# One PSUM bank per kind of product, one small product per tick, and state sums in four parts

## The chip, the cores and the metric

One core of one Trainium2 chip. The metric is the device time of the whole program in microseconds. Of the kernel before, three runs are shown: median 8285.81 us, 8284.54 to 8287.15. The chip's engines are called PE (TensorE, matmuls), DVE (VectorE), ACT (ScalarE), POOL (GpSimd) and SP (SyncE, which issues nearly all DMAs here). PSUM has eight banks of 128 partitions by 512 fp32.

## The reference, cut to what matters

Sixteen images of 64 channels by 64x64 pixels go through two layers.

```python
# layer 0
y = leaky_relu(conv3x3(x)); y = leaky_relu(conv3x3(y))
seq = y as 4096 tokens of 64 channels
x, z = split(seq @ in_proj_w)                 # 128 channels each
x = silu(conv1d(x))                           # 4 taps along the tokens
dt, B, C = split(x @ x_proj_w)                # 4, 16, 16
delta = softplus(dt @ dt_proj_w + dt_proj_b)
h = exp(delta * A) * h + (delta * x) * B      # a scan over 4096 tokens, 128 channels x 16 states
y = sum over states of h * C, + x * D
seq = (y * silu(z)) @ out_proj_w              # back to 64 channels
# layer 1
out_c = softmax(xc @ xc.T) @ x                # attention over channels
out_s = v @ softmax(q.T @ k).T                # attention over 4096 x 4096 positions
out   = x + w_bn @ concat(out_c, out_s)
```

## The kernel before, in words

The convolutions run first, by themselves, up to about 590 us. The rest is one software pipeline written out by hand, in **ticks**. An image is 8 chunks of 512 tokens. A chunk has 16 ticks, one for each group of 8 channels x 16 states, and so an image has 128 ticks. `T` counts ticks, and `r = T % 16` is the place in the chunk. In this text "r8" means the tick with r = 8 in each chunk. The 16 images are run as two spans of eight (`SPANS`), with a barrier between them. Each engine has its own loop over T, and takes its work in the order of that loop; semaphores tie the loops together.

In a tick T these things are done:

- SP fetches `lanes` for tick T+3 (`AHEAD`): 512 KB of `delta` and `delta*x`, spread over partitions (line 755). It waits for the slot of tick T-1 to be free.
- ACT takes `exp` of the lanes into `dA` for tick T+1 (line 1042). DVE multiplies lanes by B into the bank `DBU` (line 1159, "dbu" below), and scans (line 1170) into a ring `hst` of 24 slots. POOL multiplies the state of the tick before by C (line 1264, `hc_in`).
- The **search** for the largest score runs one image behind the scan: PE makes two products from keys and queries, `dif` and `max` (line 868). ACT takes a Relu of `dif` into `gains` (line 988), and DVE folds `max` and `gains` into a running maximum (line 1113), one tick after the Relu. Four key blocks of an image are loaded into `kx` (`SEARCH_LOAD`, line 709). The last of them needs the last chunk's keys, which `st_split` stores (lines 769 and 771).
- The **attention** runs `MAIN` ticks behind: PE makes two score products `S` (line 936), ACT takes their `exp` into `pr` (line 1036), PE multiplies the `pr` of the tick before by the values ("PV", line 947, eight instructions) and in every even tick sums two ticks' `pr` ("SUM", line 962, eight instructions).

Besides, each chunk needs **small products** of PE, each read by ACT or DVE: `xin` and `z` (lines 888, 890, 886), `dt` (894), `BC` (898), `y` (the sum of the states over 16 slots, 32 instructions, line 909), `out` (904), `xv` (917) and `en` (922). Every 32 ticks there are `turn` (874) and `res` (882), and once an image `mix` (878). `small_uses(T)` says which fall in a tick; before, `y` is in r2 as one block, and r0 holds both `xin` and `z`.

Five banks (`RING`) are handed out in turn to all of these, in the order in which PE writes them: `bank_of` is `number[e] % RING`. PE waits for the reader of the product five places before. Within a tick, `plan(T)` gives PE the order `dif`, S, S, `max`, PV, SUM, small products. ACT begins a tick with the Relu of `dif`, then the two `exp` of S, then `dA`, then waits for that tick's small products. DVE's further work of a chunk stands after `max` in its ticks: the gates (lines 1181 and 1186), the softplus (1192, 1194 in r7; 1200, 1203 in r9), the key difference (1209 in r8), the low part of the keys and queries (1215 in r10), and every 32 ticks `accs` (1221), the multiplication by the reciprocal (1231) and `res` (1135). ACT's `Ln` in r8 is between two loads of its function table.

The softplus result goes through `spread_d` in DRAM (`st_sp`, lines 729 and 732), and B and C through `bc_d` (`st_bc`, `ld_b`, `ld_c`, lines 738 to 746).

Of the kernel before, what the change touches and what calls it, by code (L numbers as in the profile page):

```python
# [19 lines left out]
ALU = mybir.AluOpType  # L20
# [3 lines left out]
P = 128  # L24
# [17 lines left out]
BLOCK = 32  # L42
# [68 lines left out]
class Span:  # L111
# [7 lines left out]
    def __init__(self, j, images, tail):  # L119
# [4 lines left out]
        self.uses, self.number, self.freed = [], {}, {}  # L124
        self.counts = {}
        for T in range(self.first, self.last):
# [70 lines left out]
    def small_uses(self, T):  # L197

        ev = []
        found, last = self.searches(T), self.searches(T - 1)  # L200
        if found:
            ev.append(("dif", found, (T - SEARCH) % KT))
        if last:
            ev.append(("max", last, (T - 1 - SEARCH) % KT))
# [3 lines left out]
        a = self.channel(T, MAIN + 14)  # L208
        if a is not None:
            ev.append(("mix", a))  # L210
        done = self.ended(T - 13)
# [3 lines left out]
        for name in {0: ("xin", "z"), 6: ("dt",), 10: ("BC",)}.get(r, ()):  # L215
            if self.chunk(sl + 1):
                ev.append((name, sl + 1))
        name = {2: "y", 7: "out", 12: "xv", 14: "en"}.get(r)
        if name and self.chunk(sl - 1):
            ev.append((name, sl - 1))  # L220
        return ev

    def plan(self, T):

        uses = self.small_uses(T)
        plan = [e for e in uses if e[0] == "dif"]
# [7 lines left out]
        return plan + [e for e in uses if e[0] not in ("dif", "max")]  # L234
# [203 lines left out]
def pipeline(nc, banks, seq_d, scratch, w_z, w_x_t, cw, cb, w_dt_t, w_dt, dt_b, w_bc, a_log, skip,  # L438
# [4 lines left out]
    with ExitStack() as ctx:  # L443
# [143 lines left out]
        def span(j, images, tail, i):  # L587
# [33 lines left out]
            def bank_of(e):  # L621
                return RB[number[e] % RING]
# [12 lines left out]
            for T in range(sched.first, sched.last):  # L635
# [13 lines left out]
                if sched.chunk(c):  # L649
                    for at, n in ((4, "tanh"), (5, "z_tanh"), (5, "gated"),  # L650
                                  (6, "z_gated"), (6, "abs_in"), (6, "em_in"), (7, "em1_in"),
                                  (8, "ln_in"), (9, "delta_in"), (9, "du_in"), (10, "st_sp"),
                                  (11, "st_bc"), (12, "ld_b"), (12, "ld_c")):
                        if r == at:
                            sched.note(n, c)
                if r == 6 and sched.chunk(c + 2):
# [5 lines left out]
                if sched.chunk(c):  # L662
                    for at, n in ((4, "y2_in"), (8, "st_x1"), (8, "kd_in"), (9, "head_in"),
                                  (10, "low_in"), (14, "st_split"), (13, "st_vt")):
                        if r == at:
                            sched.note(n, c)
                for n, offset in (("max_in", TURN - 1), ("nm_in", TURN), ("nm_row", TURN + 1), ("acc_in", MAIN + KT),
# [20 lines left out]
            with nc.Block() as block:  # L688
                @block.sync
                def _(sp):  # L690
# [29 lines left out]
                    for T in range(first, last):  # L720
                        sl, r = T // GROUPS, T % GROUPS
                        c = sl + 1
                        if r == 6 and sched.chunk(c + 2):
                            full_wait(sp, ("z", c))
                            load_seq(c + 2)
                        if sched.chunk(c) and r == 10:
                            if due("delta_in", c):
                                sp.wait_ge(S["delta_in"], due("delta_in", c))
                            issued(sp.dma_start(spread_d[c % 2, :, 0, :], dsp[:]), "st_sp")
                            if due("du_in", c):  # L730
                                sp.wait_ge(S["du_in"], due("du_in", c))
                            issued(sp.dma_start(spread_d[c % 2, :, 1, :], usp[:]), "st_sp")
                        if sched.chunk(c) and r == 11:
                            taken(sp, ("BC", c))
                            wait(sp, "ld_b", c - 2, 16)
                            wait(sp, "ld_c", c - 2, 16)
                            for j in range(BLOCKS):
                                issued(sp.dma_start(bc_d[c % 2][:, P * j:P * (j + 1)],
                                                    bcs[BLOCK * j:BLOCK * (j + 1), :]), "st_bc")
                        if sched.chunk(c) and r == 12:  # L740
                            wait(sp, "st_bc", c, 16 * BLOCKS)
                            wait(sp, "dbu_in", GROUPS * (c - 1) - 1)
                            issued(sp.dma_start(bbc[:, c % 2, :], bc_d[c % 2, 0:D_STATE].unsqueeze(1).broadcast_to(
                                [D_STATE, DL, CHUNK])), "ld_b")
                            wait(sp, "hc_in", GROUPS * (c - 1) - 1)
                            issued(sp.dma_start(cbc[:, c % 2, :], bc_d[c % 2, D_STATE:].unsqueeze(1).broadcast_to(
# [575 lines left out]
```

## Time and profile before

| | us |
|---|---|
| median of three runs | 8285.81 |
| the profiled execution: its own time | 8273.81 |
| the profiled execution: span of its instructions | 8272.0 |
| convolutions and loading, up to the first scan | 591 |
| scans alone (first image) | 591 to 1079 |
| scans, search and attention together | 1079 to 7843 |
| attention of the last image, and the end | 7843 to 8272 |

The page gives busy shares of the whole span: PE 91%, DVE 77%, ACT 70%, POOL 41%. Its line of the granted TensorE clock, in 40 slices of 207 us and in tenths of full speed, shows 8, 6, 6, 8 in the third to the sixth slice and 9 in all others. A matmul's end is modelled, so the starts of matmuls are what to read, not their busy time. In a row of the timeline the numbers are the start in us, how long the group took, and in brackets how long the engine had stood idle, and what ended that.

### The profile page before, as it was taken

How to read it: one execution, taken by the hardware profiler on the slowest of the kernel's cores; microseconds unless marked ns; L12 is line 12 of the kernel's file. 1: busy time of each engine (PE TensorE's matmuls, PEld its weight loads, DVE VectorE, ACT ScalarE, POOL GpSimd, SP SyncE). 2: the span in 40 equal slices, each digit the busy share in tenths (PEclk: the TensorE clock that was granted, in tenths of full speed). 3: DMA queues.
4: the chain of work that ended last, by engine and by line, in shares of the span. 5: the costliest groups of instructions: out<-in, count | busy, mean ns of one | idle time of the engine just before them, and what ended most of it. 6: DMA issues, size and time to landing. Idle time of an engine off the chain costs nothing. (4 is left out here: it accounts for less than half of the span.)

```text
span 8272.0 us, 143757 instructions
## 1 busy us (share of the span) xinstructions
PE 7526.8 (91%) x44622; PEld 2839.9 (34%) x44622; DVE 6384.9 (77%) x10331; ACT 5779.3 (70%) x10216; POOL 3397.1 (41%) x4134
## 2 busy tenths in 40 slices
PE   9963489999999999999989999999999999999999
PEld 2321133333333333333333333333333333333333
DVE  2228888888888888888878888888888888888831
ACT  1124477777877778777777777777778777787765
POOL 0015544444444444444444444444444444444400
PEclk9986689999999999999999999999999999999999
DMA  9838878888787878787877888788787878888710
GB/s 152 134 91 218 222 198 203 208 201 207 196 209 202 200 201 205 203 207 200 204 187 201 206 204 208 195 205 207 200 206 195 209 200 202 204 201 203 184 36 12
DMA packets 856720, 1555.81 MB, mean 188 GB/s; under 512 B 401288, under 2 KB 419472, under 8 KB 855952
## 3 DMA queue, kind: packets, MB, share of 16 engines
q1 hardware_dynamic: 853904, 1546.08, 76.2%
q8 instruction: 355, 5.82, 0.3%
q14 instruction: 413, 3.38, 0.2%
q10 hardware_dynamic: 2048, 0.53, 0.0%
HBM read 1335.21 MB, written 193.74 MB: 185 GB/s over the span
## 5 line engine op out<-in xcount | busy, mean ns | idle before, releaser
L1264 POOL TENSOR_TENSOR hst<-hst,cbc 128x512 f32<-128x512 f32 x2048 | 2618.2, 1278 | 3575.8 <-DVE bank L1159 3553.5
L1170 DVE TENSOR_TENSOR_SCAN hst<-dA,carry,bank 128x512 f32<-128x512 f32 x1792 | 2294.2, 1280 | 142.6 <-issue 36.6
L1036 ACT ACTIVATE pr<-bank 128x512 f32<-128x512 f32 x4096 | 2224.3, 603 | 40.2 <-PE bank L936 38.8
L947 PE MATMUL bank<-pr,vt 128*32 128x512 f32 x16384 | 2244.9, 621 | 0.0
L868 PE MATMUL bank<-kx,qr 96*128 96x512 f32 x4096 | 2046.6, 501 | 201.3 <-DMA kx<-kx_d 90.8
L988 ACT ACTIVATE gains<-bank 128x512 f32<-128x512 f32 x2048 | 1222.3, 597 | 994.3 <-PE bank L868 702.3
L1042 ACT ACTIVATE dA<-lanes,small 128x512 f32<-128x512 f32 x2048 | 1502.5, 734 | 524.5 <-DMA lanes<-spread_d 492.6
L1159 DVE TENSOR_TENSOR bank<-lanes,bbc 128x512 f32<-128x512 f32 x2048 | 1517.7, 741 | 264.3 <-DMA lanes<-spread_d 237.9
L1113 DVE CUSTOM_DVE_ANT_0 gains<-bank,gains 128x512 f32<-128x512 f32 x2048 | 1371.0, 669 | 388.5 <-PE bank L868 382.2
L936 PE MATMUL bank<-qr,kr 98*128 98x512 f32 x4096 | 1392.4, 413 | 184.3 <-ACT pr L1036 164.2
L868 PEld LDWEIGHTS bank<-kx,qr 96*128 96x128 f32 x4096 | 782.0, 191 | 1597.4 <-issue 1003.9
L962 PE MATMUL bank<-pr,ones 128*32 128x512 f32 x8192 | 1130.8, 625 | 16.6 <-ACT dens L1051 15.9
L936 PEld LDWEIGHTS bank<-qr,kr 98*128 98x128 f32 x4096 | 784.4, 192 | 529.2 <-ACT pr L1036 287.1
L947 PEld LDWEIGHTS bank<-pr,vt 128*32 128x32 f32 x16384 | 324.9, 108 | 702.4 <-issue 692.4
L909 PE MATMUL bank<-hst,cst 128*32 128x512 f32 x4096 | 481.9, 612 | 64.6 <-POOL hst L1264 64.6
L962 PEld LDWEIGHTS bank<-pr,ones 128*32 128x32 f32 x8192 | 274.3, 115 | 690.2 <-issue 624.4
L1257 POOL COPY carry<-hst 128x1 f32<-128x1 f32 x1792 | 473.4, 264 | 66.6 <-DVE hst L1170 60.5
L407 ACT ACTIVATE biased<-bank,bias 128x512 f32<-128x512 f32 x128 | 81.0, 684 | 452.9 <-PE bank L395 442.5
L1151 DVE SCALAR_TENSOR_TENSOR ysb<-u,small,bank 128x512 f32<-128x512 f32 x128 | 95.5, 746 | 390.6 <-PE bank L909 390.6
L1170 DVE TENSOR_TENSOR_SCAN hst<-dA,bank 128x512 f32<-128x512 f32 x256 | 312.5, 1221 | 11.7 <-ACT dA L1042 0.5
L1277 POOL TENSOR_TENSOR usp<-dsp,u 128x512 f32<-128x512 f32 x128 | 211.8, 1655 | 266.2 <-DVE dsp L1203 266.2
L909 PEld LDWEIGHTS bank<-hst,cst 128*32 128x32 f32 x4096 | 136.1, 114 | 395.1 <-issue 394.4
(114 smaller groups left out, 5118.9 us busy)
## 6 DMA issues: line engine op xcount, KB each, us to landing
lanes<-spread_d SPq DMA_DIRECT2D x2048, 512.0 KB, 6.4
seqt<-seq_d SPq DMA_DIRECT2D x256, 128.5 KB, 4.9
spread_d<-dsp SPq DMA_DIRECT2D x128, 256.0 KB, 2.0
spread_d<-usp SPq DMA_DIRECT2D x128, 256.0 KB, 2.0
bbc<-bc_d SPq DMA_DIRECT2D x128, 256.0 KB, 3.9
cbc<-bc_d SPq DMA_DIRECT2D x128, 256.0 KB, 4.5
kx<-kx_d SPq DMA_DIRECT2D x192, 128.0 KB, 4.8
qr<-parts_d SPq DMA_DIRECT2D x192, 128.0 KB, 4.8
```

The source lines that it names most:

```text
L868: mm = nc.tensor.matmul(bank[:].rearrange("p (c n) -> p c n", n=HALF), qr[0:SPLIT, ring_slot((a, q)), nt * P:(nt + 1) * P].bitcast(F32R), ...
L909: mm = nc.tensor.matmul(bank[BLOCK * j:BLOCK * (j + 1), :], cst[:, C_SUM + BLOCK * gl:C_SUM + BLOCK * (gl + 1)], hst[:, slot_of(GROUPS * c ...
L936: nc.tensor.matmul(bank[:], kr[0:rows, t * P:(t + 1) * P].bitcast(F32R), qr[0:rows, ring_slot((a, q)), cols].bitcast(F32R), start=True, st ...
L947: mm = nc.tensor.matmul(ACC[CH * h + o:CH * h + o + BLOCK, :], vt[:, t, o:o + BLOCK], pr[:, T % PRING, h, :], start=t == 0, stop=t == KT - ...
L962: mm = nc.tensor.matmul(DEN[o:o + 32, :], ones[:], pr[:, (2 * p + par) % PRING, h, :], start=t == 1, stop=t == KT - 1, tile_position=(0, o))
L988: nc.scalar.activation(gains[:, k % 2, :], bank_of(e)[:], ACT.Relu).then_inc(S["act_took"], 1)
L1036: nc.scalar.activation(pr[:, T % PRING, h, :], bank_of(("S", T, h))[:], ACT.Exp).then_inc(S["p_full"], 1)
L1042: nc.scalar.activation(dA[:, (T + 1) % 2, :], lanes[:, (T + 1) % SLOTS, 0, :], ACT.Exp, scale=amat[:, g:g + 1]).then_inc(S["da_in"], 1)
L1113: nc.vector.tensor_tensor_reduce(out=gains[:, k % 2, :], in0=bank[:], in1=gains[:, k % 2, :], scale=1.0, scalar=LOWEST, op0=ALU.add, op1=A ...
L1159: nc.vector.tensor_tensor(DBU[:], lanes[:, T % SLOTS, 1, :], bbc[:, sl % 2, :], ALU.mult).then_inc(S["dbu_in"], 1)
L1170: nc.vector.tensor_tensor_scan(hst[:, slot_of(T), :], dA[:, T % 2, :], DBU[:], carry[:, g:g + 1] if sl % CHUNKS else 0.0, ALU.mult, ALU.ad ...
L1264: nc.gpsimd.tensor_tensor(h, h, cbc[:, (T - 1) // GROUPS % 2, :], ALU.mult).then_inc(S["hc_in"], 1)
```

## The change

It does four things.

1. `bank_index` gives each kind of product a bank of its own: `dif` 0, `max` 1, the two S 2 and 3, all small products 4. PE waits for the reader of the product that was in the bank before (`prior`).
2. At most one small product stands in a tick, and its reader (ACT or DVE) takes it in the next tick. The new places: `xin` r1, `z` r2, `out` r3, `dt` r4, `xv` r5, `BC` r6, `en` r7, `res` or `turn` r8, `mix` r9. ACT begins a tick with the small product of the tick before, then the two `exp`, then the Relu. PE begins a tick with S.
3. `y` is written in four parts, eight instructions each, in r13, r14, r15 and r0, into one bank; DVE reads the sum in r1.
4. What follows moves along: gates r3 and r4, softplus r6 and r8, key difference r5, `head` r6, low part r7, `Ln` r7, the stores `st_bc` r8, `st_sp` and `st_split` r9, loads of B and C r10. SP fetches `lanes` before anything else of a tick. `MAIN` goes from 32 to 30, the search from -6 to -9, and the last `kx` load from tick 16 to tick 9 of the next image, where it stands behind the `st_split` of the same tick.

```diff
-MAIN = 32
-SEARCH = -6
+MAIN = 30
+SEARCH = -9
-END = 14
+RES = 10
+MIX = 57
+END = RES + 2
+SPLIT_AT = 9
-SEARCH_LOAD = [SEARCH - KT + 8 * (p + 1) + 1 for p in range(QUARTERS - 1)] + [GROUPS]
+SEARCH_LOAD = [SEARCH - KT + 8 * (p + 1) + 1 for p in range(QUARTERS - 1)] + [SPLIT_AT]
...
-                self.number[e] = len(self.uses)
-                self.uses.append(e)
+                self.number[e] = len(self.number)
+                self.prior[e] = held.get(bank_index(e))
+                held[bank_index(e)] = e
+                if e[0] == "y" and e[2] < GPB - 1:
+                    continue
...
-        for name in {0: ("xin", "z"), 6: ("dt",), 10: ("BC",)}.get(r, ()):
-            if self.chunk(sl + 1):
-                ev.append((name, sl + 1))
-        name = {2: "y", 7: "out", 12: "xv", 14: "en"}.get(r)
+        name = {1: "xin", 2: "z", 4: "dt", 6: "BC"}.get(r)
+        if name and self.chunk(sl + 1):
+            ev.append((name, sl + 1))
+        name = {3: "out", 5: "xv", 7: "en"}.get(r)
         if name and self.chunk(sl - 1):
             ev.append((name, sl - 1))
+        c, part = (sl - 1, GPB - 1) if r == 0 else (sl, r - GROUPS + GPB - 1)
+        if 0 <= part and self.chunk(c):
+            ev.append(("y", c, part))
+        assert len(ev) <= 1
         return ev
...
-        uses = self.small_uses(T)
-        plan = [e for e in uses if e[0] == "dif"]
-        if self.attends(T):
-            plan += [("S", T, 0), ("S", T, 1)]
-        plan += [e for e in uses if e[0] == "max"]
+        plan = [("S", T, 0), ("S", T, 1)] if self.attends(T) else []
+        plan += self.search_uses(T)
         if self.attends(T - 1):
             plan.append(("PV", T - 1))
         if T % 2 == 0 and self.attends(T - 1):
             plan.append(("SUM", T // 2 - 1))
-        return plan + [e for e in uses if e[0] not in ("dif", "max")]
+        return plan + self.small_uses(T)
+
+def bank_index(e):
+    return {"dif": 0, "max": 1, "S": 2 + e[-1] if e[0] == "S" else 0}.get(e[0], 4)
...
             def bank_of(e):
-                return RB[number[e] % RING]
+                return RB[bank_index(e)]
...
-                        if number[e] >= RING:
-                            taken(pe, sched.uses[number[e] - RING])
+                        if sched.prior[e]:
+                            taken(pe, sched.prior[e])
...
-                            wait(pe, "hc_in", GROUPS * (c + 1) - 1)
-                            for gl in range(GPB):
-                                for j in range(BLOCKS):
...
+                            gl = e[2]
+                            wait(pe, "hc_in", GROUPS * c + BLOCKS * (gl + 1) - 1)
+                            for j in range(BLOCKS):
...
@@ ACT, one tick
-                        near = [e for e in sched.small_uses(T) if e[0] == "dif"]
-                        for e in near:
-                            small_use(e)
+                        for e in sched.small_uses(T - 1):
+                            if e in number:
+                                small_use(e)
                         if sched.attends(T):
...
+                        for e in sched.search_uses(T):
+                            small_use(e)
                         if sched.spreads(T + 1):
...
-                        for e in sched.small_uses(T)[len(near):]:
-                            small_use(e)
```

## Rows read from the trace of the kernel before

**Rows 1.** Busy time by stage: us, then each engine, granted clock, DMA share, GB/s.
```profile
591.00:1079.00 488.00, 195.40 (x682) 81.22 (x682) 403.83 (x493) 221.55 (x335) 270.09 (x320) 0.62 0.87 219
1079.00:7843.00 6764.00, 6393.21 (x38247) 2449.67 (x38248) 5736.16 (x9328) 5225.91 (x9278) 3114.59 (x3772) 0.97 0.81 202
7843.00:8272.00 429.00, 408.09 (x2586) 146.69 (x2585) 109.45 (x305) 240.30 (x456) 3.82 (x3) 0.98 0.09 23
```

**Rows 2.** Timeline of DVE over one chunk: the scans of r4, r7 to r13.
```profile
4017.96 1.28 DVE L1170 TENSOR_TENSOR_SCAN hst<-dA,carry,bank 128x512 f32<-128x512 f32 x1
...
4027.42 1.28 DVE L1170 TENSOR_TENSOR_SCAN hst<-dA,carry,bank 128x512 f32<-128x512 f32 x1
...
4031.01 1.28 DVE L1170 TENSOR_TENSOR_SCAN hst<-dA,carry,bank 128x512 f32<-128x512 f32 x1
...
4034.10 1.28 DVE L1170 TENSOR_TENSOR_SCAN hst<-dA,carry,bank 128x512 f32<-128x512 f32 x1
...
4037.95 1.28 DVE L1170 TENSOR_TENSOR_SCAN hst<-dA,carry,bank 128x512 f32<-128x512 f32 x1
...
4042.10 1.28 DVE L1170 TENSOR_TENSOR_SCAN hst<-dA,carry,bank 128x512 f32<-128x512 f32 x1
...
4045.38 1.28 DVE L1170 TENSOR_TENSOR_SCAN hst<-dA,carry,bank 128x512 f32<-128x512 f32 x1
...
4047.89 1.28 DVE L1170 TENSOR_TENSOR_SCAN hst<-dA,carry,bank 128x512 f32<-128x512 f32 x1
```

**Rows 3.** Timeline of PE over the same chunk, from `y` in r2 to r12.
```profile
4010.36 3.62 PE L909 MATMUL bank<-hst,cst 128*32 128x512 f32 x32
...
4016.38 0.64 PE L936 MATMUL bank<-qr,kr 98*128 98x512 f32 x2
...
4019.38 0.63 PE L936 MATMUL bank<-qr,kr 98*128 98x512 f32 x2
...
4021.51 0.64 PE L936 MATMUL bank<-qr,kr 98*128 98x512 f32 x2
...
4025.37 0.63 PE L936 MATMUL bank<-qr,kr 98*128 98x512 f32 x2
...
4034.51 0.51 PE L936 MATMUL bank<-qr,kr 98*128 98x512 f32 x1 [0.24 <-ACT gains L988]
4036.42 0.79 PE L936 MATMUL bank<-qr,kr 98*128 98x512 f32 x1 [1.40 <-ACT pr L1036]
...
4037.63 1.94 PE L947 MATMUL bank<-pr,vt 128*32 128x512 f32 x8
...
4040.36 0.39 PE L898 MATMUL bank<-u,wbc 128*32 128x128 f32 x8
...
4042.71 0.38 PE L874 MATMUL bank<-cst,mx 128*8 128x128 f32 x2
...
4043.36 0.63 PE L936 MATMUL bank<-qr,kr 98*128 98x512 f32 x2
```

**Rows 4.** Waits from 1079 to 7843 us: total us, times, longest.
```profile
DVE ysb L1151 <- PE bank L909: 379.5, 117, 7.0
...
ACT xv L1024 <- PE bank L917: 94.1, 86, 1.5
...
PE bank L868 <- DMA kx<-kx_d: 80.6, 14, 7.7
```

**Rows 5.** PE's timeline after one of those waits for `kx`.
```profile
4253.51 0.77 PE L868 MATMUL bank<-kx,qr 96*128 96x512 f32 x1 [6.12 <-DMA kx<-kx_d]
```

**Rows 6.** Waits of SP's queue, 1079 to 7843 us: total, times, longest.
```profile
SPq L729 <- DVE dsp L1203: 605.6, 117, 5.7
...
SPq L604 <- DMA kx_d<-low: 72.1, 13, 6.2
```

**Rows 7.** The page's list of DMA issues: KB each, median us to landing.
```profile
lanes<-spread_d SPq DMA_DIRECT2D x2048, 512.0 KB, 6.4
```

**Rows 8.** Waits from 591 to 1079 us, scans alone.
```profile
DVE bank L1159 <- DMA lanes<-spread_d: 70.0, 25, 12.1
```

More of the change, by code:

```diff
@@ L199, in small_uses @@
         ev = []
[L200 to L204, printed above, removed]
         turned = self.quarter_at(T, TURN)
@@ L649, in span @@
                 if sched.chunk(c):
[L650 to L653, printed above, removed]
+                    for at, n in ((2, "tanh"), (3, "z_tanh"), (3, "gated"),
+                                  (4, "z_gated"), (5, "abs_in"), (5, "em_in"), (6, "em1_in"),
+                                  (7, "ln_in"), (8, "delta_in"), (8, "du_in"), (9, "st_sp"),
+                                  (8, "st_bc"), (10, "ld_b"), (10, "ld_c")):
                         if r == at:
                             sched.note(n, c)
-                if r == 6 and sched.chunk(c + 2):
+                if r == 4 and sched.chunk(c + 2):
                     sched.note(f"seq{c % 2}", c + 2)
@@ L721, in _ @@
                         sl, r = T // GROUPS, T % GROUPS
[L722 to L736, printed above, removed]
-                            for j in range(BLOCKS):
[L738 to L746, printed above, removed]
-                                [D_STATE, DL, CHUNK])), "ld_c")
                         X = sched.fetches(T)
@@ L756, in _ @@
                                                 near.partition_broadcast(D_STATE)), f"lanes{X % SLOTS}")
+                        c = sl + 1
+                        if r == 4 and sched.chunk(c + 2):
+                            full_wait(sp, ("z", c))
+                            load_seq(c + 2)
+                        if sched.chunk(c) and r == 9:
+                            if due("delta_in", c):
+                                sp.wait_ge(S["delta_in"], due("delta_in", c))
+                            issued(sp.dma_start(spread_d[c % 2, :, 0, :], dsp[:]), "st_sp")
+                            if due("du_in", c):
+                                sp.wait_ge(S["du_in"], due("du_in", c))
+                            issued(sp.dma_start(spread_d[c % 2, :, 1, :], usp[:]), "st_sp")
+                        if sched.chunk(c) and r == 8:
+                            taken(sp, ("BC", c))
+                            wait(sp, "ld_b", c - 2, 16)
+                            wait(sp, "ld_c", c - 2, 16)
+                            for j in range(BLOCKS):
+                                issued(sp.dma_start(bc_d[c % 2][:, P * j:P * (j + 1)],
+                                                    bcs[BLOCK * j:BLOCK * (j + 1), :]), "st_bc")
+                        if sched.chunk(c) and r == 10:
+                            wait(sp, "st_bc", c, 16 * BLOCKS)
+                            wait(sp, "dbu_in", GROUPS * (c - 1) - 1)
+                            issued(sp.dma_start(bbc[:, c % 2, :], bc_d[c % 2, 0:D_STATE].unsqueeze(1).broadcast_to(
+                                [D_STATE, DL, CHUNK])), "ld_b")
+                            wait(sp, "hc_in", GROUPS * (c - 1) - 1)
+                            issued(sp.dma_start(cbc[:, c % 2, :], bc_d[c % 2, D_STATE:].unsqueeze(1).broadcast_to(
+                                [D_STATE, DL, CHUNK])), "ld_c")
                         c = sl - 1
@@ L1060, in _ @@
                         c = sl + 1
-                        if sched.chunk(c) and r == 4:
+                        if sched.chunk(c) and r == 2:
                             taken(act, ("xin", c))
@@ L1076, in _ @@
                             nc.scalar.activation(em[:], em[:], ACT.Exp, scale=-1.0).then_inc(S["em_in"], 1)
-                        if sched.chunk(c) and r == 8:
+                        if sched.chunk(c) and r == 7:
                             if due("em1_in", c):
@@ L1081, in _ @@
                         c = sl - 1
-                        if sched.chunk(c) and r == 9:
+                        if sched.chunk(c) and r == 6:
                             wait(act, "kd_in", c)
@@ L1103, in small_use @@
                         kind, c = e[0], e[1]
-                        if kind not in DVE_USES or kind == "y":
+                        if kind not in DVE_USES or e not in sched.freed:
                             return
@@ L1128, in small_use @@
                                                     ALU.subtract).then_inc(S["nm_in"], 1)
+                        elif kind == "y":
+                            full_wait(dve, ("out", c - 1))
+                            nc.vector.scalar_tensor_tensor(out=ysb[:], in0=u[:, c % 2, :], scalar=dskip, in1=bank[:],
+                                                           op0=ALU.mult, op1=ALU.add).then_inc(S["dve_took"], 1)
                         elif kind == "mix":
@@ L1205, in _ @@
                         c = sl - 1
-                        if sched.chunk(c) and r == 8:
+                        if sched.chunk(c) and r == 5:
                             qk = x1c[CH:P, c % 2, :]
@@ L1210, in _ @@
                                                     ALU.subtract).then_inc(S["kd_in"], 1)
-                        if sched.chunk(c) and r == 10:
+                        if sched.chunk(c) and r == 7:
                             if due("head_in", c):
@@ L1266, in _ @@
                         c = sl - 1
-                        if sched.chunk(c) and r == 4:
-                            taken(pool, ("y", c))
+                        if sched.chunk(c) and r == 2:
+                            taken(pool, ("y", c, GPB - 1))
                             wait(pool, "z_gated", c)
@@ L1272, in _ @@
                         c = sl + 1
-                        if sched.chunk(c) and r == 9:
+                        if sched.chunk(c) and r == 8:
                             if due("delta_in", c):
```

69 lines of the change are left out of this document (33 added, 36 removed).

## The prediction

> **What bounds the kernel now.** I read the busy time by stage first, then the rhythm of the scans on DVE, then the starts of PE's matmuls over the same chunk, and last the waits.
>
> By stage, 6764 of the 8272 us belong to the stretch where scan, search and attention run together [rows 1]. It holds 118 chunks of 16 ticks, so only what happens once a chunk, or once an image there (14 images), can move the time much. PE is busy for 95% of it, DVE for 85%, ACT for 77%; DMA stands at 81%. Three things are near their limit together.
>
> The timelines say how they share it. PE's plain ticks repeat exactly: 2.13 us without SUM, 3.00 with it, and 3.86 where `dt` comes on top, so `dt` is 0.87 [rows 3]. DVE's plain tick is 2.51 us (r12, the last two scans) [rows 2]. So PE is the slower one only where a tick has SUM or a large small product, and DVE where a tick has gates, softplus or key work. Before the change the two kinds of load lie in different places. `y` stands in r2 as one block of 3.62 us [rows 3], `xin` and `z` in r0: there DVE waits (379.5 us for `y` alone [rows 4]) while PE runs without a gap. From r4 to r11 it is the other way round. From the scan of r4 to that of r12 DVE takes 27.43 us [rows 2]; PE's S of the same ticks are 26.98 us apart. PE's own work in these eight ticks is 4 x 3.00 + 4 x 2.13, `dt` and `out` at 0.87 each, `BC` and `turn` at no more than 0.39 and 0.38: 23.0 us [rows 3]. So DVE asks for 4.4 us more than PE, and PE loses 4.0 of them. The slack of about one tick between the engines takes up only 0.4. The loss shows in r10: S stands 0.24 and 1.40 us behind ACT's reads, and then the PV takes 1.94 us [rows 3].
>
> Once an image PE waits 5.8 us for the last `kx` (80.6 us in 14 waits [rows 4]), and the products after it run slow (0.77 us for one search product [rows 5], where two of S, as wide, take 0.63 [rows 3]); with that I call it 7.5 us an image.
>
> **The change part by part.** All sums go against the profiled execution, 8273.81 us.
>
> *Small products of a chunk.* PE issues the same instructions, DVE too, so 51 us of PE work in a chunk stay. What changes is where they meet. `y` costs 3.62 / 4, about 0.9 us, in each of r13, r14, r15 and r0; these ticks and r1 to r4 are now PE's. The ticks in which DVE has more to do are r5 to r9. From the spacing of the scans before [rows 2]: the key difference makes a tick 3.09 us, the first half of softplus 3.59, the second half 3.85, the low part 4.15 (with the reduction of the maximum, which comes in every other chunk; 4.0 without half of it). In r8 `en` is read too, and in every other chunk the reciprocal is multiplied in: I add 0.2 and half of 0.67 (half of what the two operations of the second softplus tick cost, 3.85 - 2.51). In r9 `res` or `turn` is read, 0.7 over 2.51. The sum of r5 to r9 is 3.09 + 3.59 + 4.0 + 4.4 + 3.2 = 18.3 us.
> PE in r5 to r9 has 3 x 2.13 + 2 x 3.00, `xv` at about 0.9, `BC` 0.4, `en` 0.6 (both `xv` and `en` are estimates between `BC` and `dt`), and half of 0.87 + 0.38 for `res` or `turn`: 14.9 us. The excess is 3.4 us. If 0.4 is taken up as before, PE loses 3.0 instead of 4.0 in a chunk. The ends: all of a tick's slack (2.1) could be used, which leaves 1.3; or ACT's table load for `Ln`, now in r7 with `head`, the gates and `xv` in the ticks around it, holds S of r9 longer and the loss stays at 4. I take 3.0, the ratio the rows show.
>
> *Readers in the next tick.* ACT stood 94.1 us behind `xv` [rows 4], 0.8 a chunk, with `dA` of the tick after queued behind it, for which DVE's scan waits. This goes: 0.6 a chunk, between 0 and 0.8. What is late next is the `exp`, which stands behind the read of the small product, but that product ended a tick's S earlier.
>
> So a chunk gains 1.0 + 0.6 = 1.6 us, 118 of them 189 us.
>
> *A bank for each kind.* PE may no longer run five products ahead; each kind must be read before its next tick. In plain ticks this costs nothing: ACT has read S some 1.5 us before PE wants the bank again, under PV. Its cover is gone where ACT is late, which is r8 and r9; there S comes first, and `dif` cannot pass in front of it as it did in r10. That is 0 to 0.5 us a chunk, which the ratio above has in it.
> The Trainium skill, "Perfetto Trace Analysis", section "Matmuls", says that independent matmul groups should rotate through different PSUM banks so that the reading of one overlaps the next group's matmuls. The change does the opposite within a kind. By that rule alone the 1.0 us of r5 to r9 would not come; the trace before, though, has its longest gap just where the ring of five rotates [rows 3]. It is the second rival.
>
> *`y` in parts.* Its first three parts need states that are many ticks old. The last needs POOL's product of r15, which runs while DVE does the dbu and scan of r0; PE comes to it at the end of r0, some 2 us later. Nothing is added, and DVE's wait in r3 goes, but under PE's work, so it buys nothing by itself.
>
> *SP's queue and the last `kx`.* SP waits 605.6 us for the softplus (5.2 a chunk) with the fetch of `lanes` for r13 behind it [rows 6]. In the new order that fetch still stands behind `st_sp`, and now behind four stores of `st_split` too, but the softplus is a tick earlier. `lanes` land 6.4 us after issue [rows 7], and three ticks of about 3 us give 9, so 2.6 us are left; I take 0 for an ordinary chunk.
> The `kx` wait of PE goes: the load is issued in tick 9 for a product of tick 15, some 18 us. But SP must stand there for `st_split` before it can issue the load; this wait is 5.5 us each today (72.1 in 13 [rows 6]), and now the fetch for r13 is queued behind it. 5.5 and 1 for the issues, less the 2.6 that are left: 4 us an image, between 0 (the stores land faster where fewer DMAs run) and 7.5. I take 4, so 3.5 an image are gained, 14 x 3.5 = 49 us.
>
> *First image.* DVE waits 70 us for `lanes` there [rows 8], and DMA stands at 0.87 [rows 1]. The new SP order, without the waits for B and C ahead of the fetch, should give a part: 0 to 40 us, I take 18 (a quarter).
>
> *Start and end.* Two ticks fewer of scan alone (488 / 160 = 3.05 us) and of attention alone (429 / 160, about 2.6, as the end's DMA chain is in it), two more of both together (3.5): 4 us.
>
> Sum: 189 + 49 + 18 + 4 = 260, so 8014 us for an execution like the profiled one. The median of the three runs lies 12 us above that one; 8026, and I say **8025**.
>
> **The rivals.**
>
> *PE's losses nearly vanish.* If the separate banks let all of a tick's slack be used, PE loses 1.3 instead of 4.0: 2.7 + 0.6 = 3.3 a chunk, 389 us, with 49 + 22 more: 460, **7825**. For it: PE loses only where a reader is late, and slow PV after the gap adds to it. Against it: 4.0 of 4.4 were lost so far.
> The Trainium skill, "Perfetto Trace Analysis", section "Identifying the Most-Contended Engine", would go further: matmul busy time is a bad measure, weight loads a good one, and these are busy for 36% of the stretch [rows 1]. By it PE would not be a limit. The exact 2.13 and 3.00 us of PE's ticks speak against it.
>
> *The separate banks give nothing.* PE stands before S of r9 as long as before, and only the `kx` wait, the first image and the ends remain: 49 + 22 = 71, **8215**.
>
> *The fetch for r13 comes late in every chunk.* Place: SP's tick 9, where spread stores, split stores and, right behind, the loads of B and C are put in front of `lanes`. Price: from the point where `lanes` take more than 9 us to land, instead of 6.4, DVE and ACT stand, and after 1.4 us of idle PE also runs slow, as in r10 before (the PV of 1.94 [rows 3]). At 2.7 us a chunk net of the 1.6 gained, 1.1 x 118 = 130, and with `kx` and the first image gaining nothing: **8415**. For it: DMA is at 81%, and SP's `kx` wait shows a store that landed slowly [rows 6]. Against it: the scan's tick before r13 leaves 2.6 us, and DMA runs nearly empty while SP waits for the softplus.
>
> *It doesn't do what it says*: the `kx` wait only moves, and the rest cancels: about 8280.
>
> **How the numbers follow.** Forecast (7890 to 8140) 0.50; losses nearly vanish 0.16; nothing from the banks (8140 to 8269) 0.16; no change 0.05; late fetch 0.13. A change of under 0.2% (17 us) can't be told from none here. Faster: 0.50 + 0.16 + 0.16 = 0.82; same 0.05; slower 0.13. The range for 8 in 10 leaves out the late fetch and the far end of the first rival: 7770 to 8250. The forecast's own range is 7890 to 8140.
>
> **What would show it.** DVE's wait for `y` gone, PE's wait for `kx` gone, PE's S in r13 to r4 spaced by its own work (3.86 in r14 and r0, 3.0 in r13 and r15), and one gap left, in r9, of 1 to 2 us before S. SP waits for `kx_d` in tick 9 of an image, and `lanes` for r13 of that chunk late. Wrong, if DVE or ACT wait for `lanes` at r13 in every chunk, if PE waits at `xin` in r1 for DVE's read of `y`, or if the gap at r9 is longer than 3 us.

## The result, and the profile after

The changed kernel takes 8208.24 us (median of four runs, 8202.77 to 8212.31) against 8285.17 for the kernel before beside it: ratio 0.9909, 95% interval 0.9894 to 0.9924. It is faster, by 0.9%, where 3.1% were forecast (8025 us). The forecast's sign was right, but of the 260 us that it gave, 77 came. The profiled execution took 8212.31 us, 61.5 less than that of before.

Busy time by stage after (us, then each engine as busy time and instructions, granted clock, DMA share, GB/s), against [rows 1]:
```profile
588.00:1079.00 491.00, 222.17 (x693) 72.52 (x693) 398.67 (x492) 220.79 (x335) 269.17 (x316) 0.57 0.86 218
1079.00:7791.00 6712.00, 6384.75 (x38292) 2431.72 (x38289) 5681.32 (x9335) 5174.91 (x9286) 3050.69 (x3777) 0.98 0.81 204
7791.00:8210.00 419.00, 399.21 (x2537) 143.92 (x2535) 105.76 (x297) 236.59 (x449) 3.52 (x3) 0.98 0.09 24
```
The borders are the same events as before: the first scan, the first S, the last scan. The common stage is 52 us shorter, with two ticks more in it. The scans alone gain nothing: the first S stands at 1079 us as before, so 158 ticks take 491 us, 3.11 each, where 160 took 488, 3.05 each. The end is some 9 us shorter.

Waits after from 1073 to 7780 us (in us: total, times, longest), against [rows 4]. Before, the same view gave 167.9 us in 128 waits for DVE behind `lanes`, and 295.8 in 266 for ACT.
```profile
ACT dA L1058 <- DMA lanes<-spread_d: 629.9, 267, 8.0
DVE bank L1170 <- DMA lanes<-spread_d: 471.8, 242, 7.2
PE bank L950 <- ACT pr L1050: 231.1, 195, 5.4
PE bank L882 <- DVE mxp L1127: 62.8, 70, 1.1
DVE ysb L1145 <- PE bank L923: 1.5, 1, 1.5
ACT xv L1038 <- PE bank L931: 0.6, 1, 0.6
```
DVE's wait for `y` (379.5 us) and ACT's for `xv` (94.1) are gone, and no wait of PE for `kx` is left. In their place DVE and ACT wait for `lanes`, some 300 us more each. 242 waits in 118 chunks are two a chunk: the timeline has them at the starts of r13 and r14, on average 1.68 and 1.72 us of DVE's idle time in a chunk that does not begin an image. ACT's rows of one chunk (start, duration, what was done, idle time before it and what ended it):
```profile
4015.22 1.28 ACT L1094 ACT_TABLE_LOAD   x1
4016.51 0.63 ACT L1094 ACTIVATE em<-em 128x512 f32<-128x512 f32 x1
4017.16 1.28 ACT L1050 ACT_TABLE_LOAD   x1
...
4033.01 0.72 ACT L1058 ACTIVATE dA<-lanes,small 128x512 f32<-128x512 f32 x1 [2.42 <-DMA lanes<-spread_d]
...
4037.04 0.72 ACT L1058 ACTIVATE dA<-lanes,small 128x512 f32<-128x512 f32 x1 [1.85 <-DMA lanes<-spread_d]
```
SP's queue in tick 9 of the same chunk says why (start, issue time, what is issued):
```profile
4019.11 0.34 SPq L752 DMA_DIRECT2D spread_d<-dsp  x1
...
4020.85 0.34 SPq L755 DMA_DIRECT2D spread_d<-usp  x1
...
4021.29 0.55 SPq L783 DMA_DIRECT2D parts_d<-head  x1
4021.89 0.55 SPq L783 DMA_DIRECT2D parts_d<-low  x1
4022.47 0.58 SPq L785 DMA_DIRECT2D kx_d<-head  x1
4023.10 0.43 SPq L785 DMA_DIRECT2D kx_d<-low  x1
4023.64 0.81 SPq L743 DMA_DIRECT2D lanes<-spread_d  x1
4024.54 1.26 SPq L766 DMA_DIRECT2D bbc<-bc_d  x1
4025.86 0.95 SPq L769 DMA_DIRECT2D cbc<-bc_d  x1
```
The four stores of the split come between `usp` and the fetch for r13 and take 2.35 us of issue; B and C follow at once. The fetch itself goes out 2.8 us after its slot is free (5.46 before), but it lands 9.34 us after its issue (4.75 before), and `dA` reads it as soon as it has landed, 9.35 us after the issue (6.24 before); these are averages over chunks that don't begin an image. The page's medians over all ticks hide this, except for B's load, which took 3.9 us before:
```profile
lanes<-spread_d SPq DMA_DIRECT2D x2048, 512.0 KB, 6.7
bbc<-bc_d SPq DMA_DIRECT2D x128, 256.0 KB, 9.5
```
PE in r8 to r11, the part that the forecast was to improve [rows 3], and the granted clock (the third value from the end) over the gap:
```profile
4013.89 0.73 PE L950 MATMUL bank<-qr,kr 98*128 98x512 f32 x2
...
4019.11 0.99 PE L950 MATMUL bank<-qr,kr 98*128 98x512 f32 x2 [1.52 <-ACT pr L1050]
...
4021.09 1.94 PE L961 MATMUL bank<-pr,vt 128*32 128x512 f32 x8
...
4022.96 1.06 PE L950 MATMUL bank<-qr,kr 98*128 98x512 f32 x2
...
4026.26 0.73 PE L950 MATMUL bank<-qr,kr 98*128 98x512 f32 x2
```
```profile
4013.50:4019.20 5.70, 4.07 (x31) 1.54 (x29) 5.53 (x12) 5.62 (x8) 1.31 (x2) 1.00 0.67 175
4019.20:4021.00 1.80, 1.80 (x4) 0.64 (x4) 0.77 (x2) 1.80 (x5) 1.75 (x2) 0.80 0.48 164
4021.00:4023.00 2.00, 2.00 (x10) 0.24 (x9) 1.93 (x5) 1.71 (x4) 1.44 (x2) 0.50 0.39 138
```
From S of r8 to that of r11 PE takes 12.37 us, for 8.5 us of work: 3.9 are lost, where 4.0 were lost before. Averaged over ordinary chunks (neither the first nor the second of an image) it is 3.6 for 3.85. PE waits at two places there: 1.25 us for ACT before S of r9, in every chunk, and 0.9 us for DVE's maximum in r10, in 56 chunks of 89.

### The profile page after: what moved, and what is told of

Same layout as the page of the kernel before. It is cut to its first block and busy times, and to the rows that moved or that the text cites. A ratio compares the mean times of both kernels' runs of the same rounds, so it can differ in the third digit from the quotient of the medians.

```text
span 8210.5 us, 143761 instructions
## 1 busy us (share of the span) xinstructions
PE 7535.5 (92%) x44622; PEld 2809.7 (34%) x44622; DVE 6321.3 (77%) x10331; ACT 5724.2 (70%) x10216; POOL 3332.0 (41%) x4134
## 5 line engine op out<-in xcount | busy, mean ns | idle before, releaser
L950 PE MATMUL bank<-qr,kr 98*128 98x512 f32 x4096 | 1724.9, 494 | 240.5 <-ACT pr L1050 231.1
L1170 DVE TENSOR_TENSOR bank<-lanes,bbc 128x512 f32<-128x512 f32 x2048 | 1497.3, 731 | 559.7 <-DMA lanes<-spread_d 536.7
L882 PE MATMUL bank<-kx,qr 96*128 96x512 f32 x4096 | 1444.9, 424 | 105.3 <-DVE mxp L1127 92.8
L1002 ACT ACTIVATE gains<-bank 128x512 f32<-128x512 f32 x2048 | 1249.2, 610 | 29.7 <-DVE mxp L1127 20.1
L950 PEld LDWEIGHTS bank<-qr,kr 98*128 98x128 f32 x4096 | 684.1, 192 | 1591.5 <-issue 865.9
L976 PE MATMUL bank<-pr,ones 128*32 128x512 f32 x8192 | 1087.9, 603 | 0.0
L923 PE MATMUL bank<-hst,cst 128*32 128x512 f32 x4096 | 569.9, 630 | 168.0 <-POOL hst L1274 142.5
L1267 POOL COPY carry<-hst 128x1 f32<-128x1 f32 x1792 | 388.0, 217 | 109.1 <-DVE hst L1181 87.8
L1036 ACT ACTIVATE cacc<-bank,small 128x512 f32<-128x512 f32 x128 | 87.9, 687 | 222.9 <-PE bank L904 221.2
```

What stands on the lines that cost most here:

```text
L882: mm = nc.tensor.matmul(bank[:].rearrange("p (c n) -> p c n", n=HALF), qr[0:SPLIT, ring_slot((a, q)), nt * P:(nt + 1) * P].bitcast(F32R), ...
L923: mm = nc.tensor.matmul(bank[BLOCK * j:BLOCK * (j + 1), :], cst[:, C_SUM + BLOCK * gl:C_SUM + BLOCK * (gl + 1)], hst[:, slot_of(GROUPS * c ...
L950: nc.tensor.matmul(bank[:], kr[0:rows, t * P:(t + 1) * P].bitcast(F32R), qr[0:rows, ring_slot((a, q)), cols].bitcast(F32R), start=True, st ...
L976: mm = nc.tensor.matmul(DEN[o:o + 32, :], ones[:], pr[:, (2 * p + par) % PRING, h, :], start=t == 1, stop=t == KT - 1, tile_position=(0, o))
L1002: nc.scalar.activation(gains[:, k % 2, :], bank_of(e)[:], ACT.Relu).then_inc(S["act_took"], 1)
L1170: nc.vector.tensor_tensor(DBU[:], lanes[:, T % SLOTS, 1, :], bbc[:, sl % 2, :], ALU.mult).then_inc(S["dbu_in"], 1)
```

## The experiments

Two theories stood against each other. A: the fetch of `lanes` for r13 lands late in every chunk, because SP's queue has the split stores in front of it and B and C right behind. B: the fixed banks give nothing, and PE is held in r9 whatever the loads do. C and D concern what holds r9: ACT (table loads, `head`) or DVE's excess of work. In the texts of what was expected, E and F are two views of the banks, G and H two of what makes the fetch late. Ratios are against the kernel before on the same chip, in brackets the 95% interval.

**Split stores two ticks later** (the last `kx` load goes with them).
```diff
-SPLIT_AT = 9
+SPLIT_AT = 11
```

> The changed kernel with the four split stores (and the last kx load behind them) in tick 11 instead of 9, so that the fetches of lanes for r13 and r14 go ahead of them. Theory A (lanes late): PE loses some 1.5 to 2 us a chunk at r13 to r15 because lanes for r13 and r14 stand behind the stores and the loads of B and C; with the stores out of the way DVE's wait for lanes falls by a third or more and the time to 8090, between 8050 and 8150. Theory B (banks and table load): the loss is the gap before S of r9, the waits for lanes lie beside it and cost nothing: 8208 within 15 us.

8021.09 us, 0.9692 (0.9677 to 0.9706): 2.2% better than the change itself, by one number. The waits of the common stage:
```profile
ACT dA L1058 <- DMA lanes<-spread_d: 247.1, 141, 7.2
DVE bank L1170 <- DMA lanes<-spread_d: 203.3, 109, 7.5
```
Theory A, and larger than it said. DVE's gaps at r13 and r14 are gone; PE's S in r13 and r14 follow at 2.98 and 3.84 us, the work of those ticks, where the change had 3.69 and 4.75 (over all chunks). DVE stands 1.0 us at r15 instead, but in an ordinary chunk PE's S follows there at 3.05 us, close to its own work.

**B and C three ticks later**, and both together.
```diff
-                                  (8, "st_bc"), (10, "ld_b"), (10, "ld_c")):
+                                  (8, "st_bc"), (13, "ld_b"), (13, "ld_c")):
-                        if sched.chunk(c) and r == 10:
+                        if sched.chunk(c) and r == 13:
```

> The changed kernel with the loads of B and C (512 KB) in tick 13 instead of 10. Theory A: lanes for r14 no longer stand behind them, r14's wait (1.7 us on DVE) goes and r13's stays: 8110, between 8070 and 8160. Theory B: 8208 within 15 us.

> Both moves together. Theory A: DVE's waits for lanes at r13 and r14 fall to under 0.5 us each, PE's S ticks there come down to their own work (3.0, 3.9, 3.0), 8030, between 7980 and 8080. Theory B: 8208 within 15 us.

8163.08 us, 0.9865 (0.985 to 0.9879), just above theory A's range, and with the split stores in r11 too 8071.58, 0.9752 (0.9737 to 0.9766). Alone it brings a fifth of what moving the stores does. Together it is worse than moving the stores alone: B and C then come late for r0, and DVE stands 0.9 us there in r1. Alone, r14's wait falls from 1.7 us to 0.05 and r13's stays at 1.6, as theory A has it, but 0.6 us come up in r1; so what B and C cost behind the fetch shows only net of what they cost when they are late themselves. Moving what stands in front of the fetch is what pays.

**Lanes fetched four ticks ahead**, in five slots, with one buffer of `zs` less to make room. The slots and `zs` buffers begin at zero again in the second half of the images, so there some `lanes` and `zs` are read from the wrong buffer; the work is the same.
```diff
-SLOTS = 4
-AHEAD = 3
+SLOTS = 5
+AHEAD = 4
...
-        zs = sb("zs", [P, 4, CHUNK])
+        zs = sb("zs", [P, 3, CHUNK])
```

> The changed kernel with lanes fetched four ticks ahead into five slots instead of three into four (zs has three buffers instead of four, to make room). Nothing of the order on SP changes but the fetch's tick. Theory A: a whole tick (some 3 us) more for lanes to land covers the lateness of 1.7 us in ordinary chunks and most of the 5 us once an image: 7980, between 7930 and 8040. Theory B: 8208 within 15 us.

7993.45 us, 0.9666 (0.965 to 0.9682), as expected, with the stores left where the change put them:
```profile
ACT dA L1058 <- DMA lanes<-spread_d: 216.3, 143, 5.4
DVE bank L1170 <- DMA lanes<-spread_d: 166.7, 106, 5.2
```
It is the lead of that fetch that is short, then. Two different edits give it, and either brings the time to where the forecast was.

**Is it bytes or places in the queue?** The first variant with four stores of 16 KB, of a constant, in front of the fetch in tick 9.
```diff
+                            if r == 9:
+                                for n in range(4):
+                                    issued(sp.dma_start(dummy_d[n], cst[CH:P, 0:64]), "st_dummy")
```

> The kernel with the stores in tick 11 (8021), and in tick 9, where the stores stood, four stores of 16 KB each of a constant to a scratch tensor, 64 KB in all instead of 384. Theory G (lanes for r13 are late because SP spends 2.3 us on issuing four more DMAs ahead of the fetch): about half of the 187 us comes back, 8110, between 8060 and 8200. Theory H (the 384 KB ahead of lanes on the DMA engines do it): 8021 to 8045.

8222.96 us, 0.9922 (0.9905 to 0.9938): all of the first variant's gain is lost again, which is beyond both expectations. SP's queue, and the waits:
```profile
4025.03 2.41 SPq L781 DMA_DIRECT2D dummy_d<-cst  x4
4027.55 0.55 SPq L744 DMA_DIRECT2D lanes<-spread_d  x1
```
```profile
ACT dA L1062 <- DMA lanes<-spread_d: 596.7, 228, 9.4
DVE bank L1174 <- DMA lanes<-spread_d: 484.1, 161, 9.6
```
But the place of the wait moved. The `lanes` of r13 now come in time (4.85 us from issue to landing, 6.68 to use); those of r15 come 3.3 us late, since the loads of B and C and the real split stores stand 2.4 us later in the queue. So 2.4 us of SP's issue time cost as much as the change's stores did. In r13 it is the load of the real stores that counts: behind four stores of 384 KB in all the fetch took 9.34 us to land, behind four of 64 KB 4.85, with none 4.92. Whether the bytes do it or the number of rows, one run doesn't split. The Trainium skill ("Perfetto Trace Analysis", section "What \"DMA-bound\" means") counts a solid sequencer track of the issuing engine as a bound of its own; the trace agrees for this stretch, where SP issues almost without a break from 4025.03 to 4033.71 us, though not for the kernel as a whole.

**The same in the kernel before:** its split stores in r11 instead of r14, the last `kx` load in tick 13 instead of 16, nothing else.
```diff
-SEARCH_LOAD = [SEARCH - KT + 8 * (p + 1) + 1 for p in range(QUARTERS - 1)] + [GROUPS]
+SEARCH_LOAD = [SEARCH - KT + 8 * (p + 1) + 1 for p in range(QUARTERS - 1)] + [13]
...
-                                  (10, "low_in"), (14, "st_split"), (13, "st_vt")):
+                                  (10, "low_in"), (11, "st_split"), (13, "st_vt")):
-                            if r == 14:
+                            if r == 11:
```

> The kernel before with one part of the change: split stores in tick 11 instead of 14, and the last kx load in tick 13 of the next image instead of 16, two ticks behind the stores; it is needed in tick 18. If the wait is worth 5.5 to 7.5 us an image, as predicted: 80 to 105 us less, 8180, between 8165 and 8200. If it only moves into SP's queue: 8273 within 15.

8809.22 us, 1.0633 (1.0617 to 1.0649); both expectations missed. PE's `kx` wait is gone, as meant, and this came instead:
```profile
ACT dA L1042 <- DMA lanes<-spread_d: 700.7, 153, 7.9
DVE bank L1159 <- DMA lanes<-spread_d: 491.8, 117, 6.1
```
Four stores in front of the fetch for r15, in every chunk, cost 4.2 us of DVE each time, to save a wait that comes once an image. It is the fault of the change, made in the kernel before and three times as dear.

**Only the banks**, in the kernel before.
```diff
-                return RB[number[e] % RING]
+                return RB[bank_index(e)]
...
-                        if number[e] >= RING:
-                            taken(pe, sched.uses[number[e] - RING])
+                        if sched.prior[e]:
+                            taken(pe, sched.prior[e])
```

> The kernel before with nothing but the bank of its own for each kind of product; places, readers and order as before. The prediction gave this part 0 to 0.5 us a chunk of cost where ACT is late. But xin and z share a tick there, and z must now stand until ACT has read xin at the end of its own tick. Theory E (a bank of its own only works with one small product a tick): PE loses about 2 us more in r0 and DVE behind it, 8450, between 8350 and 8600. Theory F (the banks themselves bring the gain): 8190 or less.

8631.43 us, 1.0422 (1.0404 to 1.0439). That is more than either theory had. With several small products in a tick, PE stands in front of the second until the first is read (`z` behind `xin` in r0); the search product `dif` waits for the reader of its own bank as well, which it did not do before; and DVE's wait for `y` grows from 379.5 to 453.4 us:
```profile
PE bank L875 <- ACT gains L995: 127.2, 184, 1.2
PE bank L893 <- ACT cacc L1029: 98.0, 117, 0.8
DVE ysb L1158 <- PE bank L916: 453.4, 117, 7.0
```
The rule of the Trainium skill that I weighed ("Perfetto Trace Analysis", section "Matmuls") holds here: without the rotation the kernel takes 4.2% longer. In the change it doesn't bite, as one small product a tick leaves each a tick to be read: PE's longest wait for a small product's reader is 7.6 us in all (for `y`). So the separate banks need the new places. Whether the new places alone, with the ring of five kept, would do as well, no run shows.

**What holds r9.** First variant, with ACT's `Ln` replaced by `Tanh`, so that no table load is needed (this changes the softplus).
```diff
-                            nc.scalar.activation(em1[:], em1[:], ACT.Ln).then_inc(S["ln_in"], 1)
+                            nc.scalar.activation(em1[:], em1[:], ACT.Tanh).then_inc(S["ln_in"], 1)
```

> The kernel with the stores in tick 11 (8021), and Tanh in place of the softplus's Ln: the output is not the reference's, but every instruction keeps its size, and ACT no longer loads its function table twice a chunk (2 x 1.28 us). In r8 to r10 PE now loses some 4.4 us a chunk. Theory C (ACT's table loads hold S of r9, and the slow clock after the gap does the rest): the loss falls by 3 to 4 us, 118 chunks, 7640, between 7550 and 7720. Theory D (as the prediction had it, DVE's excess of work in r5 to r9): DVE's work is the same, so 7960, between 7900 and 8010.

8159.53 us, 0.9853 (0.9839 to 0.9868): 1.6% slower than with the table loads, and both expectations missed. PE's rows, and the granted clock around the gap:
```profile
4038.72 0.80 PE L882 MATMUL bank<-kx,qr 96*128 96x512 f32 x1 [2.74 <-DVE mxp L1127]
4039.45 1.94 PE L961 MATMUL bank<-pr,vt 128*32 128x512 f32 x8
```
```profile
4034.00:4039.50 5.50, 2.76 (x17) 0.98 (x20) 5.39 (x8) 3.51 (x8) 3.69 (x5) 0.84 0.73 213
4039.50:4042.50 3.00, 3.00 (x17) 0.55 (x16) 2.96 (x5) 0.41 (x1) 1.90 (x3) 0.50 1.02 241
```
The gap behind ACT in r9 is gone, and one tick later PE waits for DVE's maximum instead, in one piece of 2.74 us. So both C and D are there, one behind the other. From the scan of r4 to that of r11 DVE takes 25.3 us in the first variant and 25.2 here: its excess has to be paid, and ACT's lateness mostly decides where. But PE stands idle longer, 2.7 us an ordinary chunk for 1.9, and the half clock follows the long gap in nearly every chunk: 540 us of the common stage, 269 in the first variant. DVE's next tick takes 3.92 us for 2.80, as it waits 1.15 us for PE's product in it (0.20 in the first variant); that is 1.1 of the 1.4 us that an ordinary chunk loses.

**`head` and low part three ticks later** (on top of the first variant), which takes them away from the softplus on ACT and DVE alike.
```diff
-                    for at, n in ((2, "y2_in"), (5, "st_x1"), (5, "kd_in"), (6, "head_in"),
-                                  (7, "low_in"), (SPLIT_AT, "st_split"), (7, "st_vt")):
+                    for at, n in ((2, "y2_in"), (5, "st_x1"), (5, "kd_in"), (9, "head_in"),
+                                  (10, "low_in"), (SPLIT_AT, "st_split"), (7, "st_vt")):
-                        if sched.chunk(c) and r == 6:
+                        if sched.chunk(c) and r == 9:
-                        if sched.chunk(c) and r == 7:
+                        if sched.chunk(c) and r == 10:
```

> The kernel with the stores in tick 11, and the cast of head (ACT, 0.83 us) moved from r6 to r9 and the low part (DVE, 1.4 us) from r7 to r10. Both theories of the gap in r9 give a gain, of different size: C, ACT comes to the table load 0.83 us earlier, PE's gap of 1.5 us falls to 0.7 and the slow clock after it comes less often, 1 to 2 us a chunk, 7850; D, DVE's excess in r5 to r9 falls by 1.4, about 1.2 us a chunk, 7880. No gain at all would be against both.

7953.68 us, 0.9605 (0.959 to 0.9619): 0.9% better than the first variant, half of what either theory gave. The gap splits into pieces:
```profile
4003.19 0.98 PE L950 MATMUL bank<-qr,kr 98*128 98x512 f32 x2 [0.82 <-ACT pr L1050]
4004.83 1.06 PE L961 MATMUL bank<-pr,vt 128*32 128x512 f32 x8
...
4007.49 0.50 PE L882 MATMUL bank<-kx,qr 96*128 96x512 f32 x1 [0.70 <-DVE mxp L1127]
```
In these rows the first is halved (on average 0.4 us a chunk for 1.25), waits for DVE's maximum come more often in r10 (73 ordinary chunks of 89, for 51 in the first variant) and anew in r12, and PV takes 1.06 us, no longer 1.94. PE's idle time has not fallen: it is 2.1 us an ordinary chunk, for 1.9. What fell is the half clock, from 269 us of the common stage to 55. With `Tanh` again on top of that:

> The kernel with the stores in tick 11 and head and low in r9 and r10 (7954), and Tanh in place of Ln (the softplus is not computed rightly, sizes are the same). In the run without the move, PE ran into a wait of 2.74 us for DVE's max in r10 as soon as ACT's table loads were gone. If that wait was DVE's excess of work in r6 to r9 (theory D), 1.4 us of it have been moved to r10, where PE has a SUM: no wait above 1.5 us, little slow clock, 7900, between 7850 and 7950. If the wait comes back as long, and with it the slow clock in each chunk: 8080, between 8030 and 8150.

7989.5 us, 0.9645 (0.9631 to 0.966), between the two expectations and slower than with the table loads once more: the wait for DVE's maximum in r10 is one of 1.82 us, and the PV behind it takes 1.94. PE stands idle less than with the table loads (1.9 us an ordinary chunk for 2.1), but the half clock is back, with 375 us for 55.

**`kx` load two ticks behind its stores** (on top of `head` in r9).
```diff
... + [SPLIT_AT]
... + [SPLIT_AT + 2]
```

> The kernel with the stores in tick 11 and head and low in r9 and r10 (7954), and the last kx load two ticks behind the stores, in tick 13 of an image, so that SP need not stand still for the stores to land. PE needs it in tick 15. If SP's standing still (8 us an image) costs PE 2 to 4 us an image: 7915, between 7890 and 7940. If PE now waits for kx instead: 7954 or more.

7929.08 us, 0.9572 (0.9558 to 0.9587), 0.3% better than without it, in the expected range. DVE's waits for `lanes` fall from 200.1 to 126.0 us; 31.7 us of PE's `kx` wait come back for it:
```profile
PE bank L882 <- DMA kx<-kx_d: 31.7, 15, 3.8
```

**Together:** split stores in r11, `head` and low part in r9 and r10, lanes four ahead (the later `kx` load is not in it), with slots and `zs` buffers numbered through both halves.
```diff
+    def slot(self, X):
+
+        return (X + TICKS * self.j) % SLOTS
```

> The kernel with the stores in tick 11 and head and low in r9 and r10 (7954), and lanes fetched four ticks ahead into five slots (numbered through both spans, zs in three buffers likewise). What is left of lanes waits there is some 1 us on DVE at r15 and 3 to 4 us an image. If these still cost PE time: 7900, between 7870 and 7930. If they lie beside other gaps: 7954 within 15.

7882.75 us, 0.9516 (0.9502 to 0.953), as expected: the best version, 4.8% faster than the kernel before and 4% faster than the changed one.
```profile
ACT dA L1062 <- DMA lanes<-spread_d: 30.5, 25, 2.9
DVE bank L1174 <- DMA lanes<-spread_d: 25.0, 14, 2.7
```

## Why the prediction was right or wrong

I compare the spacing of PE's S, averaged over a chunk (from r8 to the next r8). An ordinary chunk (neither the first nor the second of an image) took 56.25 us before, 56.15 after and 54.69 with lanes four ahead, each for the 51 us of PE's work that the prediction counts.

*SP's queue: the step that failed.* "`lanes` land 6.4 us after issue [rows 7], and three ticks of about 3 us give 9, so 2.6 us are left; I take 0 for an ordinary chunk." The fetch for r13 landed after 9.34 us, nothing was left, and DVE and ACT wait for `lanes` at r13 in every chunk, which I had named as a sign of being wrong. I took a median over all ticks for the one tick in which four stores stand ahead and half a megabyte of B and C behind. The term is 56.15 - 54.69 = 1.46 us a chunk, 172 us in all, where I had put nothing; with the image's chunks and the rest, lanes four ahead bring the ratio 2.4 points under that of the change, some 200 us. Two separate remedies (stores later, fetch earlier) and the same fault in the kernel before show it. It was among the rivals, with its place and its traces as they came, but priced at 2.7 us a chunk and given 0.13, for I held against it that DMA runs nearly empty while SP waits for the softplus. Before, DMA's share was 0.28 there (4033.7 to 4040.4 us). After, it is 0.58 in SP's wait (4016.4 to 4019.1 us), 0.41 up to 4023.6 us while the stores go out, and 0.85 in the 9.4 us behind, in which the fetch is to land.

*Small products of a chunk.* Forecast 1.0 us saved in r5 to r9. Measured 0.2: on average 3.6 lost for 3.85 (3.9 for 4.0 in the chunks shown). The bound that I named as an end of the range ("ACT's table load ... holds S of r9 longer and the loss stays at 4") was the case; with `head` in the same ticks ACT is 1.52 us late in the chunk shown. That DVE's excess would be there anyway was right (the two runs with `Tanh`).

*Readers in the next tick.* ACT's wait for `xv` went from 94.1 us to 0.6. The gain was larger than 0.6 us: before, an ordinary chunk lost 5.25 us, 3.85 of them between S of r4 and S of r12, so 1.4 elsewhere; with lanes four ahead it loses 3.7, all of it in r8 to r11. So 1.4 against 0.6. That all of it comes from the readers and not also from `y` in parts, no run separates. The two errors cancel, which is luck: 1.56 us a chunk against my 1.6, had `lanes` come in time.

*A bank for each kind.* Nothing was to be lost in plain ticks, and nothing is: S follows S at 2.13 us in r11 and 3.00 in r12. ACT's lead in such ticks was smaller than the 1.5 us that I gave (before, 0.4 us in r5 and 1.5 in r12), but it was enough. What held PE in r9 stayed with the ring gone, so the ring was not its cause; in the kernel before with the banks alone, PE's wait for ACT in r10 is 1.41 us a chunk, as it was with the ring (1.40).

*The last `kx`.* PE's wait is gone and SP waits for `kx_d` in tick 9 instead, as said:
```profile
SPq L752 <- DVE dsp L1216: 307.4, 117, 2.8
...
SPq L618 <- DMA kx_d<-low: 93.4, 13, 8.0
```
Forecast 7.5 us gained and 4 given back in an image. By the chunks' averages the second chunk of an image took 8.0 us more than an ordinary one before (0.2 after), and the first chunk takes 5.3 more now. 2.4 net, 34 us instead of 49.

*First image, start and end.* Forecast 18 us for the first image and 4 for start and end. In the first image nothing was gained: with two ticks fewer the first S comes no earlier, as a tick takes 3.11 us for 3.05, and DVE's wait for `lanes` from 588 to 1079 us hardly fell from [rows 8]:
```profile
DVE bank L1170 <- DMA lanes<-spread_d: 66.8, 23, 8.9
```
The late fetch has a part in this, too: with the split stores in r11 the same 158 ticks take 475.5 us, with lanes four ahead 474.1. The end gave 9 us.

*Together:* 0.1 x 118 = 12 and 34 for `kx` make 46 us of the common stage. Between the same two ticks (S of T = 160 and S of T = 2047) the change takes 62 us less; I have not followed up the other 16, which lie in the first and last chunks and in the rounding of the averages. S of T = 160 comes 10 us later than before, and the end is 9 shorter: 61.5 us, by which the profiled executions differ.

*A rival's number, not its account.* 8208 us is close to the 8215 of "the separate banks give nothing", and its condition held: PE's gap before S of r9 stayed. That the numbers meet is chance. By that account no more was to be had in an ordinary chunk; the runs show that 1.56 us a chunk were there, and that the late fetch took them back.

## What to carry to other kernels

A median landing time is no price for the one transfer that is issued in a crowd: when a step moves, list what the queue issues just ahead of and just behind the most urgent fetch in that tick, and compare its lead with the landing time there. Give the fetch that everything waits for one more slot, or move bulk stores behind it, before changing anything finer. Where two limits lie behind each other, removing the first may make things worse, so a gap should be shortened on both engines together.

## What the runs showed of the hardware that was not expected

Waiting less on ACT made the kernel slower twice, as the wait behind it then came in one piece of 2.74 or 1.82 us. PE's idle time alone does not say which run is faster. The first variant has 1.9 us of it in an ordinary chunk and 269 us at the half clock in the common stage. With `head` moved it is 2.1 and 55, and the kernel is faster; with `Tanh` on top of that 1.9 and 375, and it is slower again. The first variant with `Tanh` has 2.7 and 540, and is the slowest of the four.
